# Preparation of the quantised cross attention: first blocks begun in the fourth sublayer's last slots, clearings and subtractions on GpSimd

## The reference

```python
x = x + jnp.tanh(g_ffn[1]) * _L1_ffn_ref(_layernorm(x), ...)     # fourth sublayer
x = x + jnp.tanh(g_xattn[2]) * _L2_xattn_ref(_layernorm(x), ctx_2048, Wq, bq, Wkv, bkv, Wp, bp)   # fifth

q = (x @ Wq + bq).reshape(1, B * N, 16, 16) / sqrt(16)           # all 1024 rows are one sequence
k, v = split of (cond @ Wkv + bkv)                               # 1024 keys, 16 heads of 16
q, k = _fq_sym(q, axis=-1), _fq_sym(k, axis=-1)                  # rounded to 127 steps for each row and head
v = _fq_sym(v, axis=2)                                           # one step for each channel, over all 1024 rows
attn = _fq_unsigned(softmax(q @ k.T), axis=-1)                   # 255 steps
out = (attn @ v) @ Wp + bp
```

## Time and profile before

| | |
|---|---|
| median of 3 runs (lowest, highest) | 1603.11 us (1602.96, 1610.41) |
| the profiled execution | 1606.58 us, span 1604.8 us |
| PE busy | 1264.0 us, 79% |
| DVE busy | 1184.0 us, 74% |
| ACT busy | 975.4 us, 61% |
| POOL busy | 287.3 us, 18% |
| granted TensorE clock, mean | 0.895 |

### The profile page before, as it was taken

One profiled execution on the slowest core, in us unless ns is written; L12 is line 12 of the kernel. 1 busy time (PEld: TensorE's weight loads), 2 busy tenths in 40 slices (PEclk: granted clock), 3 DMA queues, 4 the chain that ended last, 5 costly groups with the idle time before them and its releaser, 6 DMA issues.

```text
span 1604.8 us, 26805 instructions
## 1 busy us (share of the span) xinstructions
PE 1264.0 (79%) x9052; PEld 917.0 (57%) x9108; DVE 1184.0 (74%) x2669; ACT 975.4 (61%) x2887; POOL 287.3 (18%) x369
## 2 busy tenths in 40 slices
PE   5774666569889799799789999657676777998898
PEld 4663344347666566576567677334444444886686
DVE  4787689868998988987534541889898988785353
ACT  2562486678778778687345661358788888332221
POOL 0000223225444354354100000000101000001000
PEclk7996677689999999999989999868798979997999
DMA  5301100100000000000510000000000000100000
GB/s 216 151 4 40 66 0 0 43 14 1 8 1 4 3 1 7 0 1 1 200 77 1 1 1 1 20 1 1 1 0 0 0 1 1 53 0 1 1 1 27
DMA packets 13583, 38.12 MB, mean 24 GB/s; under 512 B 2201, under 2 KB 8866, under 8 KB 10802
## 3 DMA queue, kind: packets, MB, share of 16 engines
q1 hardware_dynamic: 13490, 36.99, 6.1%
HBM read 35.94 MB, written 1.05 MB: 23 GB/s over the span
## 4 chain that ended last, share of the span: by engine, by line
DVE 41%; PE 39%; issue 9%; ACT 9%; POOL 1%; DVEq 0%; DMA 0%; another core or an unknown queue 0%; SPq 0%; ACTq 0%; POOLq 0%
DVE small L2509 7%; DVE work L2519 4%; PE PS L3086 3%; DVE work L1189 2%; PE PS L1919 2%; PE PS L1403 2%; PE PS L1950 2%; PE PS L1844 2%; DVE work L1201 2%; ACT work L1385 2%; DVE small L1223 2%; DVE work L1239 2%; PE PS L368 1%; PE PS L3122 1%; PE PS L2739 1%
## 5 line engine op out<-in xcount | busy, mean ns | idle before, releaser
L2425 ACT ACTIVATE work<-PS,small 128x1024 f32<-128x1024 f32 x128 | 154.7, 1208 | 19.9 <-DVE small L2511 14.4
L2509 DVE TENSOR_REDUCE small<-PS 128x1 f32<-128x1024 f32 x128 | 155.5, 1215 | 4.8 <-PE PS L2336 4.1
L1294 POOL TENSOR_TENSOR small<-small,minus_half 128x4 f32<-128x4 f32 x96 | 104.5, 1089 | 252.1 <-ACT small L1335 252.0
L2356 PE MATMUL PS<-ident_b,work 128*128 128x128 bf16 x1024 | 91.4, 241 | 66.4 <-DVE work L2519 52.7
L1411 PE MATMUL PS<-late 128*128 128x512 f16 x384 | 103.8, 398 | 50.5 <-DVE work L1217 44.2
L213 POOL TENSOR_TENSOR rstd<-moments,eps 128x1 f32<-128x1 f32 x56 | 13.8, 246 | 583.5 <-DVE moments L193 583.5
L1385 ACT ACTIVATE work<-PS,small 128x128 f32<-128x128 f32 x256 | 90.5, 365 | 44.0 <-DVE small L1224 43.0
L2356 PEld LDWEIGHTS PS<-ident_b,work 128*128 128x128 bf16 x1024 | 67.0, 107 | 77.6 <-DVE work L2519 52.2
L2519 DVE TENSOR_SCALAR work<-work 128x1024 bf16<-128x1024 f32 x128 | 87.5, 684 | 12.9 <-ACT work L2425 11.0
L1411 PEld LDWEIGHTS PS<-late 128*128 128x128 f16 x384 | 36.0, 100 | 103.8 <-DVE work L1217 43.3
L2418 ACT COPY work<-PS 128x512 f32<-128x512 f32 x128 | 75.0, 586 | 30.6 <-PE PS L2356 30.3
(11 more groups left out here) (416 smaller groups left out, 3414.5 us busy)
## 6 DMA issues: line engine op xcount, KB each, us to landing
late<-in_C_proj SPq DMA_DIRECT2D x1, 4096.0 KB, 12.6
ctxT<-in_ctxT SPq DMA_DIRECT2D x24, 128.0 KB, 2.6
late<-in_C_q SPq DMA_DIRECT2D x1, 2048.0 KB, 8.2
late<-in_C_qx SPq DMA_DIRECT2D x1, 2048.0 KB, 12.7
late<-in_F_w SPq DMA_DIRECT2D x2, 1024.0 KB
late<-in_B_gate SPq DMA_DIRECT2D x1, 1024.0 KB, 8.4
late<-in_B_up SPq DMA_DIRECT2D x1, 1024.0 KB, 10.2
late<-in_B_down SPq DMA_DIRECT2D x1, 1024.0 KB, 12.1
```

What stands on the lines that cost most here:

```text
L1294: return nc.gpsimd.tensor_tensor(rs, rs, minus_half[:, 0:4], ALU.pow)
L2356: last = nc.tensor.transpose(bank(g, 1).bitcast(BF16)[:, b * P:(b + 1) * P], E_[g]["pb"][:, b * P:(b + 1) * P], ident_b[:])
L2425: nc.scalar.activation(E_[g]["e"], banks(g, 2), ACT.Exp, scale=small[:, g, h:h + 1], bias=small[:, g, 48 + h:49 + h], accum_out=small[:, g ...
L2509: ch.link(nc.vector.tensor_reduce(small[:, g, 80:81], banks(g, 2), AX.X, ALU.max))
```

## The change

Blocks 0 and 1 of the context (`EARLY` = 2) are projected and rounded in the last two slots of the fourth sublayer: TensorE projects block 0 after the last up projection and block 1 at the beginning of slot 5, and VectorE rounds both in slot 5 between the last product and the addition to x. The preparation then starts with block 2, and what was tied to b = 0 to 5 is tied to b = 2 to 7. The clearings, the scaling of the output bias and all sixteen subtractions move from VectorE to GpSimd. Seven clearings wait for the last up projection, the two in a region that the down projections read wait for their end. GpSimd's third part is formed one block after the first subtraction (`less_middle(b - 1)`). The scaling of the bias and its addition to x now follow the reduction. A semaphore's second use (`E_cleared`) tells TensorE that the last clearings are done.

```diff
 slot of D_vector
                     modulated(f)
+                if f2 == STEPS - 1 and layers > 4:
+                    E_early_vector(dve, ch)
                 if f2 is not None:
                     add(f2)
...
 slot of D_tensor
+                if f2 == STEPS - 1 and layers > 4:
+                    E_early_tensor(pe, 1)
                 if f2 is not None:
                     down(f2, 2)
                     down(f2, 3)
...
                     up(f, 3)
+                if f == STEPS - 1 and layers > 4:
+                    E_early_tensor(pe, 0)
...
+        def E_early_tensor(pe, b):
+            if b == 0:
+                pe.wait_ge(weights_in[4], weights_sent[4])
+            else:
+                pe.wait_ge(D_silus.sem, D_silus.at(STEPS - 1, CHUNKS - 1))
+            E_project_kv(pe, b)
...
-            pe.wait_ge(x_done.sem, 4 * NB)
-            for b in range(NB + LAG):
+            for b in range(EARLY, NB + LAG):
                 if b < NB:
-                    project_kv(b)
+                    E_project_kv(pe, b)
                 if b >= LAG:
                     turn_kstack(b - LAG)
-                if b == 1:
+                if b == EARLY + 1:
+                    pe.wait_ge(x_done.sem, 4 * NB)
...
+        def E_early_vector(dve, ch):
+            dve.wait_ge(weights_in[4], weights_sent[4])
+            for b in range(EARLY):
+                E_rounded_k(dve, ch, b)
...
             norm_stats(ch, 0)
-            for b in range(NB + G):
-                if b < NB:
-                    rounded_k(b)
+            for b in range(EARLY, NB):
+                E_rounded_k(dve, ch, b)
...
-                if b >= G:
-                    less_middle(b - G)
-                if 0 <= b - 1 < NB:
-                    less_high(b - 1)
...
         def E_before_gpsimd(pool, ch):
-            norm_gpsimd(pool, ch, 0)
-            E_add_bias(pool, 0)
+            pool.wait_ge(D_up.sem, D_up.at(STEPS - 1, CHUNKS - 1))
+            for g in range(G):
+                ch.link(nc.gpsimd.memset(E_[g]["kstack"][:, :, 3, :], 0.0))
+                ch.link(nc.gpsimd.memset(E_[g]["stack"][:, :, 3, :], 0.0))
+                ch.link(nc.gpsimd.memset(E_[g]["qT"][ROWS:, :, :], 0.0))
+            ch.link(nc.gpsimd.memset(ones_b, 1.0))
+            for b in range(NB + 1):
+                if b < NB:
+                    less_high(b)
+                if b:
+                    less_middle(b - 1)
+                if b == 1:
+                    pool.wait_ge(D_down.sem, D_down.at(STEPS - 1))
...
+                    norm_gpsimd(pool, ch, 0)
             pool.wait_ge(E_vmax.sem, E_vmax.nth(0, 0))
             nc.gpsimd.partition_all_reduce(E_vs[:, 0, :], E_vs[:, 1, :], P, bass.bass_isa.ReduceOp.max).then_inc(E_vall, 1)
+            pool.wait_ge(weights_in[4], weights_sent[4])
+            ch.link(nc.gpsimd.tensor_scalar(E_bias[:, 3 * D:4 * D], ..., gates[:, 0, 2:3], None, ALU.mult))
+            E_add_bias(pool, 0)
```

More of the change, by code:

```diff
@@ L2087, in program @@
         E_biased = follow(B_hq)
+        E_cleared = follow(B_hqT)
         E_vs_col = root[:, 0, 40:42]
@@ L2113, in program, with E_project_kv @@
         LAG = G + 1
-        def E_before_tensor(pe, ch):
-            def project_kv(b):
-                g = b % G
-                ctx_loaded(pe, b // G, g)
-                if b >= G:
[L2121 to L2124, removed]
+        EARLY = G
+        def E_project_kv(pe, b):
+            g = b % G
+            ctx_loaded(pe, b // G, g)
+            if b >= G:
+                pe.wait_ge(E_kvread.sem, E_kvread.nth(0, b - G))
+            for k in range(KC):
+                last = nc.tensor.matmul(bank(g, 0), ctxT[:, g, k, :], wE["kv"][:, k, :], start=k == 0, stop=k == KC - 1)
+            last.then_inc(E_kv.sem, 1)
+        def E_early_tensor(pe, b):
[4 more added lines that the diff above has]
+            E_project_kv(pe, b)
+        def E_before_tensor(pe, ch):
             def turn_kstack(b):
@@ L2188, in step_of @@
             ch.link(nc.vector.tensor_scalar(s, s, 1.0 / 127, least, ALU.mult, ALU.max))
-        def E_before_vector(dve, ch):
[L2192 to L2213, removed]
-                nc.vector.tensor_tensor(heads16(e["ku"]), heads16(e["kt"]), e["kstack"][:, :, 0, :], ALU.subtract).then_inc(E_ku.sem, 1)
-            def less_middle(b):
-                e = E_[b % G]
-                dve.wait_ge(E_kmid.sem, E_kmid.nth(0, b))
-                nc.vector.tensor_tensor(e["kstack"][:, :, 2, :], heads16(e["ku"]), e["kstack"][:, :, 1, :], ALU.subtract).then_inc(E_kstack.sem, 1)
-            for g in range(G):
-                ch.mark(nc.vector.memset(E_[g]["kstack"][:, :, 3, :], 0.0))
-                ch.mark(nc.vector.memset(E_[g]["stack"][:, :, 3, :], 0.0))
-                ch.mark(nc.vector.memset(E_[g]["qT"][ROWS:, :, :], 0.0))
-                ch.mark(nc.vector.memset(E_[g]["qT_odd"][0:ROWS, :, :], 0.0))
-            ch.mark(nc.vector.memset(ones_b, 1.0))
-            ch.mark(nc.vector.tensor_scalar(E_bias[:, 3 * D:4 * D], E_bias[:, 3 * D:4 * D], gates[:, 0, 2:3], None, ALU.mult))
-            ch.restart()
@@ new lines, in E_rounded_k @@
+        def E_rounded_k(dve, ch, b):
+            g = b % G
+            e = E_[g]
+            dve.wait_ge(E_kv.sem, E_kv.nth(0, b))
+            if b >= G:
+                dve.wait_ge(E_ku.sem, E_ku.nth(0, b - G))
+            nc.vector.tensor_tensor(E_v[:, b, :], bank(g, 0)[:, D:2 * D], E_bias[:, 2 * D:3 * D], ALU.add).then_inc(ctx_read[g], 1)
+            read = nc.vector.tensor_tensor(e["kt"], bank(g, 0)[:, 0:D], E_bias[:, D:2 * D], ALU.add)
+            read.then_inc(E_kvread.sem, 1)
+            dve.wait_ge(E_kvread.sem, E_kvread.nth(0, b))
+            s, r = root[:, g, 0:16], root[:, g, 16:32]
+            step_of(ch, e["kt"], s, 1e-8)
+            ch.link(nc.vector.reciprocal(r, s))
+            ch.link(nc.vector.tensor_tensor(heads16(e["kt"]), heads16(e["kt"]), over_d(r), ALU.mult))
+            ch.link(nc.vector.tensor_scalar(e["kt"], e["kt"], MAGIC, MAGIC, ALU.add, ALU.subtract))
+            nc.vector.tensor_tensor(heads16(e["kt"]), heads16(e["kt"]), over_d(s), ALU.mult).then_inc(E_kt.sem, 1)
```

42 lines of the change are left out of this document (29 added, 13 removed).

## The result

The changed kernel took 1601.94 us (median of 16 runs, 1594.68 to 1607.49), the kernel before 1608.09 us in the runs beside it (16 runs, 1602.06 to 1621.42). The ratio is 0.9959 (0.9942 to 0.9976): 6.6 us faster, with 3.8 to 9.3 as the interval. Forecast were 9.8 us and a time of 1593.3, with a range of 1589.0 to 1601.5. So the direction and most of the gain were right, and the time lies 0.4 us outside the range. It is 8.6 us above the forecast, and two things make that up: the level was 5.0 us higher than the 1603.11 us from which I subtracted (1608.09), and the gain between the two medians is 6.15 us, 3.7 less than the 9.8.

A forecast was written before the change was run, and what follows sets the result against it. VectorE was taken to bound the first 39.6 us, a chain of short steps the next 14.5. Scaling of the values at 1044.4 + 1.0 + 0.6 + 0.9 = 1046.9, 9.8 us earlier: median 1603.1 to 1593.3 us, range 1589.0 to 1601.5.

The forecast's parts named there:

- the term behind the scaling: After the scaling of the values: the change alters nothing VectorE does, so the local gain carries over whole.
- Step 1: TensorE, last slots: two key/value projections before and between the down matmuls lie on its own path, cost 3.7 us.
- Step 2: VectorE, last slot: two 2.87 us rounding blocks fit into the idle 6.15 us; slack 0.6 us, cost nothing.
- Step 3: VectorE, addition to x until maximum over channels: the maximum starts at 1031.4 against 1042.25, 10.8 us earlier.
- the first allowance: Preparation before the scaling: VectorE and GpSimd hinder each other at the shared port, 0.6 us allowed.
- The rival in which every subtraction costs its whole length: VectorE loses the port each time: about 11 subtractions at 0.62, 6.8 us, giving 1600.1 us; chance 0.08.
- Step 4: Subtractions on GpSimd: 0.62 us each, engine loop 3.6 us per block against VectorE's 3.85, so VectorE stays the pace.
- the loop: Rival in the block preparation: ScalarE, GpSimd and TensorE become the pace, 3.8 us, giving 1597.1 us; chance 0.09.
- Steps 5 and 6: Before the scaling: VectorE ready at 1043.4; GpSimd's 5.88 us code change and 1.14 us reduction end at 1044.3 and a hop.
- The slow projection: Allowance in the preparation: one of six projections at the slow clock, 3.62 us instead of 1.84, half counted, 0.9 us.
- a change of 10.34 us: Rival ahead of the reduction: GpSimd's change of code costs 10.34 us, 4.5 us more, giving 1597.8 us; chance 0.10.
- the slower side: Rival ahead of the scaling: code change and reduction together exceed 19.4 us, 1.7 us slower, 1604.8 us; chance 0.07.

The follow-up runs named there:

- early blocks alone: Changed kernel with clearings, bias scaling and subtractions back on VectorE, only blocks 0 and 1 begun early; ratio to the kernel before 0.9993.
- clearings alone: Kernel before with only the clearings and the bias scaling moved to GpSimd, subtractions on VectorE, no early blocks; ratio to the kernel before 0.9989.
- the shortened kernel: Kernel before with VectorE work left out (maximum over one block, values unscaled, keys unrounded), no subtraction on GpSimd; last sublayer's entry 57.9 us in both traces.
- the moves to GpSimd alone: Changed kernel with no block begun early (EARLY = 0); clearings, bias scaling and subtractions on GpSimd; ratio to the kernel before 0.9945.

## Why the prediction was right in its mechanism and short in its time

**The local sum held.** Predicted were 9.8 us for the start of the scaling. The three traces of before have a stretch of 60.86, 60.26 and 61.60 us, those of the changed kernel 51.38, 51.12 and 52.28: means 60.9 and 51.6, a gain of 9.3 us.

**Failed: the carry-over to the whole, "median 1603.1 to 1593.3 us", and the term behind the scaling that it put at nothing.** The forecast took its level from three runs (1602.96 to 1610.41). The medians of the kernel before in the five timings beside other kernels are 1608.1 to 1611.2, so the level alone was 5 us too low or more, the larger part of the 8.6 us between forecast and measurement. The range allowed only for the costs of the change, not for what unchanged code does from one execution to the next: the last product, ahead of everything that the change does on VectorE, starts anywhere between 992.0 and 1002.3 us in the eighteen traces.

The sentence "From there on the change alters nothing that VectorE does" is true of the instructions, not of the time that I took from it. The scaling to the end takes 549.1 us in the mean of the five traces without subtractions on GpSimd (before three times, early blocks alone, clearings alone; 548.1 to 550.3), and 551.2 in the mean of the nine with them (549.2 to 552.8). 2.1 us come back, 1.5 of them in the entry above. 9.3 less 2.1 is 7.2, which agrees with the measured 6.6 and 8.5 of the two timings. That the two groups differ in their means is measured, though they overlap; that GpSimd's work causes it is not shown, and the shortened kernel speaks against it. The cause stays open.

**Step 1, right.** 3.7 us predicted for the two projections, 10.27 - 6.84 = 3.43 measured.

**Step 2, right in place, with less slack.** Both blocks lie ahead of the addition, and TensorE, not VectorE, ends its wait. The first block waited for its projection (1.03 us) and the second too (1.87 us).

**Step 3 and the first allowance, mis-sized.** The addition to the maximum was to take 25.05 us and took 27.67. VectorE's operations beside GpSimd's were stretched by 2.17 us where I allowed 0.6: L2223 0.29 to 0.65 three times, L2502 0.41 to 0.75, L2523 0.42 to 0.73, L2517 0.70 to 1.17. With the next term, 0.44, that is the whole difference. The wait for rstd is 0.44 us where I priced nothing: GpSimd's clearings of 0.94 us stand ahead of the norm. The rival in which every subtraction costs its whole length (6.8 us) was wrong: no operation was stretched by more than 0.47 us, and 2.17 us is 27% of the 8.0 us that the twelve subtractions there take at 0.67. The Trainium skill (SBUF — State Buffer, SBUF: two separate sides) describes the port as an exclusive lock; the trace agrees for single operations (0.65 is 0.29 and 0.36 of waiting) and shows that most of them don't meet.

**Step 4, right.** 0.62 us taken, 0.67 measured, and the loop did not become the pace: in VectorE's blocks no wait for a difference appears.

**Steps 5 and 6, right but for the hidden work.** The leg was to take 13.0 us and 1.0 of hidden work, 14.0; it took 13.44, 13.18 and 12.96. The first maximum of scores was to come 9.2 us into it and came at 9.60, 9.60 and 9.14. The slow projection, allowed 0.9 us, cost VectorE nothing in the first two traces and 0.90 in the third, in step 3. The code change cost 5.99 where 5.88 was taken, and by the Trainium skill's 5.95 (GPSIMD Engine Reference, Instruction dispatch) the sum would be the same. The added 1.0 us of work that the record does not show was wrong: VectorE went on 0.04 us after the record's end. So VectorE's 0.98 us of waiting is for the change of code and the reduction's own 1.08 us, nothing else. The rivals of a change of 10.34 us and of the slower side didn't come: the ends that they needed were not there.

**The credit within the change was wrong, though the total was not.** I had the early blocks at 3.1 us and the rest at 6.7. The traces show 8.2 for the moves to GpSimd alone, 0.9 for the early blocks alone, and 0.4 to 1.5 for them on top of the moves (52.66 against 51.12 to 52.28), where single traces scatter by 1.3. No ratio tells the changed kernel from the moves alone. The early blocks cost what I had not priced: they take two blocks of cover from the work on q, and its copies on ScalarE then stand in the last leg (16.60 instead of 14.45 us, 13.4 instead of 11.3).

## What to carry to other kernels

Price a move by the leg it shortens last: here work begun earlier took cover away from another chain (q), while the same subtractions, taken from behind a 3.6 us reduction on VectorE, paid twice. A range should hold the scatter of code that the change does not touch, which repeated runs of the kernel before show (1601 to 1621 us), and a local gain should be measured between two fixed instructions before it is carried over to the whole.

## What the runs showed that I had not expected

Small VectorE operations with one operand wait for GpSimd too. In the kernel with GpSimd alone, VectorE's row (first) and GpSimd's (second) run together:

```profile
1009.42 0.69 DVE L2201 TENSOR_SCALAR root<-root 128x16 f32<-128x16 f32 x1
```

```profile
1009.41 0.67 POOL L2267 TENSOR_TENSOR work<-work 128x256 bf16<-128x256 f32 x1
```

The same operation takes 0.17 us where GpSimd stands still. GpSimd's own are stretched as well (0.67 to 0.87 at 1022.40 in the changed kernel). The change of code ahead of the reduction took 5.73 to 6.00 us in ten traces and the way back 6.70 to 7.82, always hidden here. The 10.34 of the earlier trace rows was no chance event of one trace: the kernel's first reduction has it in all eighteen traces (9.14 to 11.21 us), the second one 5.80 to 6.20. The moved reduction never paid it; why the first does stays open.
